# A ViT tower's patch sums on Trainium2: GpSimd halves one tile of x per group in place of two, and VectorE sums the first tile whole

## The reference

```python
pooled = x.reshape(64, 12, 14, 16, 14, 16).sum(axis=(3, 5))        # 16 x 16 patch sums
h = einsum('bcij,ce->bije', pooled, channel_weights)               # 196 tokens of 192 features an image
h = h + attn(layernorm(h))      # 12 heads, causal; only the 14 tokens with the highest selection probability get it added
h = h + gelu(layernorm(h) @ in_weight.T + in_bias) @ out_weight    # 192 -> 768 -> 192
```

## Time and profile before

| what | us |
|---|---|
| median of 3 runs | 670.09 |
| lowest, highest | 669.08, 673.85 |
| the profiled execution | 671.92 |
| its span, first to last instruction | 670.2 |
| mean granted clock of TensorE | 0.949 |
| busy: TensorE, VectorE, ScalarE, GpSimd | 590.3, 508.6, 347.2, 242.1 |

### The profile page before, as it was taken

One profiled execution on the slowest core, in us unless ns is written; L12 is line 12 of the kernel. 1 busy time (PEld: TensorE's weight loads), 2 busy tenths in 40 slices (PEclk: granted clock), 3 DMA queues, 4 the chain that ended last, 5 costly groups with the idle time before them and its releaser, 6 DMA issues.

```text
span 670.2 us, 12462 instructions
## 1 busy us (share of the span) xinstructions
PE 590.3 (88%) x3912; PEld 474.7 (71%) x3912; DVE 508.6 (76%) x1110; ACT 347.2 (52%) x847; POOL 242.1 (36%) x458
## 2 busy tenths in 40 slices
PE   2568687999998999899979979989989999999995
PEld 1346374777977797768767867769777877788774
DVE  4988669797979797979888866979897888752411
ACT  2013325475656556655656445656565565646541
POOL 1022333151545245443626224533634273304001
PEclk9886586999999999999999979999999999999998
DMA  8999958889898969897897869797999884010101
GB/s 320 332 384 366 400 160 326 288 289 309 283 354 277 353 231 366 266 358 243 322 308 282 260 229 295 256 355 240 361 271 342 257 334 95 10 41 12 32 6 42
DMA packets 33461, 171.82 MB, mean 256 GB/s; under 512 B 3428, under 2 KB 17776, under 8 KB 20978
## 3 DMA queue, kind: packets, MB, share of 16 engines
q1 hardware_dynamic: 21600, 146.11, 60.4%
q0 software_dynamic: 6512, 11.01, 9.1%
q10 hardware_dynamic: 5282, 13.87, 5.6%
HBM read 158.55 MB, written 12.43 MB: 255 GB/s over the span
## 4 chain that ended last, share of the span: by engine, by line
PE 44%; DVE 19%; issue 12%; DMA 9%; POOL 8%; ACT 5%; POOLq 1%; SPq 1%; DVEq 0%; ACTq 0%
PE psO L715 16%; DVE R L1055 5%; DMA X<-in_x 5%; PE psS L670 4%; PE psF L700 3%; PE psS L647 3%; DMA patch_sums<-R 3%; PE psS L659 3%; PE psC L685 2%; PE psC L690 2%; PE psA L613 2%; DMA out<-OS,idx 2%; DVE mx L1169 2%; PE psS L653 2%; ACT SP L830 1%
## 5 line engine op out<-in xcount | busy, mean ns | idle before, releaser
L715 PE MATMUL psO<-W,act 128*112 128x192 f32 x1344 | 266.6, 336 | 7.0 <-ACT act L893 7.0
L1055 DVE TENSOR_REDUCE R<-X 128x42 f32<-128x2688 f32 (+1 forms) x111 | 258.8, 2358 | 18.2 <-POOL X L430 16.6
L715 PEld LDWEIGHTS psO<-W,act 128*112 128x112 f32 x1344 | 217.4, 180 | 25.6 <-issue 17.8
L893 ACT ACTIVATE act<-psF 128x392 f32<-128x392 f32 x192 | 95.3, 497 | 134.8 <-PE psF L700 122.1
L430 POOL TENSOR_TENSOR X<-X 128x1344 f32<-128x1344 f32 x31 | 93.9, 3032 | 13.5 <-DMA X<-in_x 13.5
L700 PE MATMUL psF<-Stk,M1S 104*128 104x392 bf16 x192 | 65.9, 343 | 8.5 <-ACT act L893 8.5
L439 POOL TENSOR_TENSOR Pt<-Praw 48x196 f32<-48x196 f32 x14 | 7.5, 536 | 153.2 <-DMA Praw<-patch_sums 153.2
L900 ACT ACTIVATE obuf<-psO 112x192 f32<-112x192 f32 x112 | 36.6, 326 | 27.8 <-PE psO L719 23.4
L659 PE MATMUL psS<-ET,F 98*64 98x336 f32 x128 | 41.9, 472 | 1.5 <-ACT ET L873 1.5
L700 PEld LDWEIGHTS psF<-Stk,M1S 104*128 104x128 bf16 x192 | 18.9, 99 | 32.9 <-ACT act L893 24.8
L670 PE MATMUL psS<-B,G 128*56 128x192 f32 x192 | 41.0, 337 | 0.0
(11 more groups left out here) (225 smaller groups left out, 929.4 us busy)
## 6 DMA issues: line engine op xcount, KB each, us to landing
X<-in_x SPq DMA_DIRECT2D x96, 1344.0 KB, 8.0
X<-in_x SPq DMA_DIRECT2D x15, 672.0 KB, 4.4
X<-in_x POOLq DMA_DIRECT2D x15, 672.0 KB, 13.5
out<-obuf ACTq DMA_DIRECT2D x16, 588.0 KB, 8.4
patch_sums<-R ACTq DMA_DIRECT2D x14, 147.0 KB, 8.4
Praw<-patch_sums ACTq DMA_DIRECT2D x14, 147.0 KB, 5.5
act<-in_x SPq DMA_DIRECT2D x1, 1344.0 KB, 18.7
W1T<-in_w1t SPq DMA_DIRECT2D x1, 576.0 KB
```

The source lines that it names most:

```text
L715: pe.matmul(to, act_sb[u % 2][:, m, i * OT:(i + 1) * OT], W2[:, m, :], start=(m == 0), stop=False)
L893: act.activation(act_sb[u % 2][:, n // 2, (n % 2) * (GT // 2):(n % 2 + 1) * (GT // 2)], psF[:, 0:GT // 2], ACT.Gelu).then_inc(act_F1.sem, 1)
L1055: dve.tensor_reduce(R[:, r, t * TQ * N:(t + 1) * TQ * N].rearrange("p (q j) -> p q j", q=TQ), v, AX.XY, ALU.add).then_inc(dve_L, 1)
```

## The change

The tuple HALVED loses tile 0, GpSimd's plan loses H:0:0, and the halving of group 1's tile 0 ahead of the plan goes. Group 0's tile 0 is still halved. `sum_tile` then reads tile 0 of groups 1 to 15 whole, and waits for its load in place of GpSimd.

```diff
-HALVED = (0, 5)
+HALVED = (5,)
...
-            plan = ("c:s:5 X:3:1 P:s:2 H:5:1 A:var2:2 K:v:2 K:d1:2 K:d2:2 H:0:0").split()
+            plan = ("c:s:5 X:3:1 P:s:2 H:5:1 A:var2:2 K:v:2 K:d1:2 K:d2:2").split()
...
             add_halves(1, 3)
-            halve(1, 0, x_halved)
             for part in ("v", "d1", "d2"):
```

## The result

The changed kernel is slower. Its median is 678.58 us (670.65 to 682.01, 20 runs), beside 672.79 us (669.07 to 675.98, 20 runs) for the kernel before on the same chip: a ratio of 1.0068, 95% interval 1.0042 to 1.0094. The prediction was 668.0 us, range 664.5 to 672.5. The profiled execution took 680.1 us (span 678.1), where that of before took 671.92 (span 670.2); these two lie 8.2 us apart, the medians 5.8. Lines from 494 on are one lower than before.

The account below looks back on a forecast made before the run. It took TensorE as nearly the bound mid-kernel, VectorE close behind. Terms -2.7 -0.3 +0.4 +0.5 = -2.1 us on the profiled 671.92 gave 669.8; that execution lies 1.8 above the median, so 668.0, range 664.5 to 672.5.

Parts of the forecast that it names:

- L1027 at the start: VectorE's first-layer weight preparation: without GpSimd's halving beside it, L1027 takes 0.96 us in place of 3.65, -2.69 us.
- VectorE's exchange: VectorE's whole tile 0 sums replace waits for GpSimd: -0.3 us over six stage C stretches, +0.4 for one uncovered stretch without.
- that cover: VectorE's nm, without stage C: it ends with GpSimd's tile 5 halving, so arriving 0.5 us later costs nothing in five stretches.
- What moves on GpSimd: GpSimd's adding DMA of tile 3 goes out 3.0 us earlier, costing +0.1 us in each of five stretches, +0.5.
- The second rival: GpSimd's moved adding DMA collides with the patch sums' store: five stretches 1.65 us longer, +8.3, giving 675.8; chance 0.06.
- The clock as a rival: TensorE's lower clock over 100 to 140 us eats or doubles the gain: 1.7 us, 669.7 or 666.3; chance 0.15.

Follow-up runs that it names:

- e2: Kernel before, with only group 1's tile 0 summed whole, GpSimd still halving tile 0 of groups 2 to 15; 668.10 us, ratio 0.9966.
- e1: Changed kernel, with tile 3's adding DMA held until VectorE has summed tile 0 of its group; 667.62 us, ratio 0.9948 to the kernel before.
- e7: Kernel before, with group 1's tile 0 summed whole and the adding DMA held until VectorE has summed tile 0; 668.72 us, ratio 0.995.
- e11: Changed kernel, with ScalarE's load of the patch sums two entries later, behind a Gelu and an output; 671.54 us, ratio 1.0028 to the kernel before.
- e6: Changed kernel without tile 3's adding DMA from group 2 on, leaving half of that tile out; 676.84 us, ratio 0.9985 to the kernel before.
- e3: Kernel before, with tile 3's adding DMA put ahead of the halving of tile 0 in GpSimd's order; 706.35 us.
- e10: Changed kernel, adding DMA held until VectorE has summed tile 0, GpSimd's tile 5 halving until tile 1 is summed; 669.57 us, ratio 0.9976 to the kernel before.

## Why the prediction was wrong, point by point

- **L1027 at the start, -2.7.** Right: 0.96 us for 3.65 in the profile, and -2.3 us in the medians of e2 (interval 0.5 to 4.2).
- **VectorE's exchange, -0.3 and +0.4.** The sum was right within about 3 us (e1 and e7 have the same ratio). The halves weren't where I put them: with C the whole tile costs about +0.4 us a stretch, where I took -0.05. nm in the stretches without C still ends with the halving of tile 5 (0.87 to 1.18 us in four, one at 0.17), so that cover held.
- **"What moves on GpSimd", +0.5. This is the step that failed.** I wrote "Nobody waits for it sooner" and "I take +0.1 us for each of five stretches". Three things in it were wrong. The place: I looked at 257.50 to 261.22, a stretch without stage C, where the adding DMA stood 3.7 us behind the store and after the move is still 0.8 to 1.3 behind; those stores stayed at 8.4 to 9.3 us. In the stretches with C it stood 1.3 to 1.7 us behind, and 2.3 to 3.0 us earlier puts it ahead. I had that distance in the trace and didn't read it. The path: I followed the late sums to GpSimd's halving at 273.36; the first to wait is ScalarE, whose load stands ahead of a Gelu. The row was in the waits of before too, 4.9 us. The price: I took a late store at its own lateness, 1.65 us at most. The stores with C came 0.15 to 2.0 us later than in the same places before, and their stretches took 0.4 to 4.5 us more, as the pause took TensorE's clock with it. In place of +0.5 the stretches with C took 14.2 us more in the profiled execution. Of these 11.3 (240.14 - 228.85) are gone in e1 and so belong to this term; the rest is about what the exchange costs there (2.6 by e1 against e7).
- **The second rival** had the mechanism (675.8, chance 0.06), but its place was wrong too, and its argument against ("the 9.90 us store had its adding DMA no earlier than the others") was about stores with nothing ahead of them, which says nothing on a DMA that comes ahead.
- **The clock as a rival, 1.7 us either way,** was looked for between 100 and 140 us. There it is 0.83 in both, and over the first 140 us it is even a little higher after, 0.82 for 0.79. It fell between 140 and 600 us instead: 0.99 before, 0.96 after, 0.99 in e1_hold. 0.03 of 460 us is 13.8 us of work, about the size of the whole loss with stage C.

The six ScalarE waits with C and their stretches, from the trace of after: 1.27 us and 36.90; 1.51 and 38.46; 1.67 and 40.59; 1.73 and 38.49; 2.65 and 44.86 (with the pause); 2.85 and 40.84. The shortest wait cost nothing that shows; in the other five stretches the clock fell. It isn't a sharp rule: before, a wait of 1.78 us at 451.15 was followed by a stretch of 36.44, and in e11 one of 1.41 us at 301.85 by 37.02.

**Open.** Why the store is late when the other DMA is ahead. The trace shows the times of both, not the order inside the DMA engines. The Trainium skill, "DMA: Bandwidth & Descriptors", section "Queues, rings and completion order", says that each DMA engine takes packets in turn from the queues that have work. By that rule the store shares with an adding DMA that is under way; the direction agrees (8.2 to 8.9 us with it 3.3 us or more behind, as in e1, 9.6 to 10.9 ahead), and no run here shows the packets. An adding DMA ahead is not the only thing that makes a store late: one store, near 320 to 330 us, took 9.90 us in before (adding DMA 3.8 us behind), 9.73 in e1 and 9.47 in e6, which has no adding DMA there at all. Also open: how e3's 36 us split, what a wait needs to take the clock along, and the +0.4 us of the exchange with stage C.

## What to carry to other kernels

When an instruction leaves an in-order engine, list every DMA behind it and read, in each kind of stretch, how far it stands from the small transfer that someone waits for; what counts is not the shift but whether it changes sides. A short wait ahead of a nearly saturated TensorE has to be priced with the clock that it may take along. And a transfer that is too early can be put right with one wait on an event that is on time anyway, as e1_hold shows.

## What the runs showed of the hardware that I had not expected

- A 147 KB store took 8.2 to 9.0 us with a 672 KB adding DMA issued 3.2 us or more behind it (e1_hold; one of 12 stores 9.7, single ones in e7 and e10 9.5), and 9.6 to 10.9 us with it 1.0 to 1.6 us ahead (after, six stores).
- In a pause of 2.27 us TensorE's granted clock fell to 1.2 GHz, stayed there for 6.8 us, and cost 3.0 us of work behind the pause, more than the pause (after, 301.3 to 308.1).
- A VectorE operation on one column, 0.16 to 0.5 us elsewhere, took 3.41 us beside a GpSimd operation of 3.01; a faster transfer upstream had moved the two onto each other.
